# The opening stage of an attention and mixture-of-depths block: modulation in columns, first key and value pieces into four banks, loads and stack copies in another order

## The reference, cut to what matters

```python
x: (8, 1024, 512); c: (8, 512); wmod: (512, 6*512)
mod = (silu(c) @ wmod).reshape(8, 6, 1, -1)
sa, ca, ga, sb, cb, gb = mod[:, 0], ..., mod[:, 5]
ga = (2 * (ga >= 0) - 1) * maximum(abs(ga), 0.25)      # gb likewise
h = layernorm(x) * (1 + ca) + sa
x = x + ga * attention(h)        # 16 "heads": q, k, v = h @ W + b, reshaped to (b, 16, 32, 1024)
                                 # scores k^T v * temperature, softmax, then q times the probabilities
h = layernorm(x) * (1 + cb) + sb
x = x + gb * ffn(h)              # half of the tokens, chosen by a router score, go through W1, gelu, W2
```

## Time and profile before

| | us |
|---|---|
| median of 3 timed runs | 2418.35 (2418.11 to 2418.71) |
| the profiled execution's own time | 2416.8 |
| its span in the trace | 2415.1 |
| PE busy | 2273.9 (94% of the span) |
| DVE busy | 1911.6 (79%) |
| ACT busy | 1478.1 (61%) |
| POOL busy | 1371.5 (57%) |

### The profile page before, as it was taken

How to read it: one execution, slowest core, us unless ns; L and a number is a source line. 1 busy time by engine, 2 the same in 40 slices (tenths; PEclk the granted TensorE clock), 3 DMA queues, 4 the chain that set the end, 5 groups by cost and what they waited for, 6 DMA issues and landing times.

```text
span 2415.1 us, 41301 instructions
## 1 busy us (share of the span) xinstructions
PE 2273.9 (94%) x12772; PEld 887.0 (37%) x12772; DVE 1911.6 (79%) x2806; ACT 1478.1 (61%) x2616; POOL 1371.5 (57%) x1205
## 2 busy tenths in 40 slices
PE   6999999999999999999999999897989999999996
PEld 2333333333333333333333333231334444444442
DVE  5899899999999999999999999998744543554432
ACT  1788888888888888888888887777311111111110
POOL 4566676666756667666666666554344452543531
PEclk9999999999999999999999999999999999999998
DMA  6233333233333333323233333223612021111100
GB/s 214 68 92 77 79 82 88 72 91 72 76 87 77 84 73 90 82 70 96 67 80 97 72 79 75 67 61 97 157 44 66 22 59 52 32 57 44 57 23 18
DMA packets 123771, 180.83 MB, mean 75 GB/s; under 512 B 44112, under 2 KB 44112, under 8 KB 123480
## 3 DMA queue, kind: packets, MB, share of 16 engines
q1 hardware_dynamic: 113760, 152.30, 25.8%
q0 software_dynamic: 9728, 25.23, 3.4%
HBM read 67.17 MB, written 43.16 MB: 46 GB/s over the span
## 4 chain that ended last, share of the span: by engine, by line
PE 64%; DVE 17%; issue 8%; POOL 5%; ACT 3%; DMA 2%; SPq 1%; DVEq 0%; POOLq 0%; ACTq 0%
PE sc L558 13%; PE acc L605 13%; PE sc L747 12%; PE sc L734 12%; DVE nmax L981 10%; PE pj L568 7%; PE pj L580 5%; POOL x L1320 3%; DVE qn L1042 2%; ACT probs L810 2%; DVE stats L1024 1%; DMA room<-in_L_ffn_W 1%; PE sc L591 1%; POOL sel_rows L120 1%; DVE rinv L1037 1%
## 5 line engine op out<-in xcount | busy, mean ns | idle before, releaser
L810 ACT ACTIVATE probs<-sc,nmax 128x1024 f32<-128x1024 f32 x1024 | 1136.7, 1114 | 276.2 <-DVE nmax L981 254.8
L981 DVE TENSOR_REDUCE nmax<-sc 128x1 f32<-128x1024 f32 x1024 | 1212.6, 1215 | 61.1 <-PE sc L558 55.1
L605 PE MATMUL acc<-probs,qn 128*32 128x512 f32 x4136 | 556.7, 611 | 9.8 <-DVE x L1019 7.3
L883 ACT ACTIVATE probs<-sc,b_col 128x512 f32<-128x512 f32 x128 | 87.9, 687 | 561.6 <-PE sc L734 498.7
L568 PE MATMUL pj<-room 128*128 128x512 f16 x1536 | 395.6, 381 | 0.4 <-ACT qT L800 0.4
L747 PE MATMUL sc<-room,probs 128*128 128x512 f16 x1536 | 353.9, 380 | 8.0 <-DVE probs L1171 8.0
L558 PE MATMUL sc<-room 128*128 128x512 f16 x1024 | 310.3, 385 | 38.3 <-ACT probs L810 27.9
L558 PE MATMUL sc<-stacks 128*128 128x512 f16 x1024 | 309.5, 384 | 31.4 <-ACT probs L810 30.8
L1169 DVE CAST probs<-probs 128x512 f16<-128x512 f32 x128 | 64.6, 505 | 332.6 <-ACT probs L883 315.9
L747 PEld LDWEIGHTS sc<-room,probs 128*128 128x128 f16 x1536 | 150.0, 98 | 190.5 <-issue 7.4
L568 PEld LDWEIGHTS pj<-room 128*128 128x128 f16 x1536 | 150.2, 98 | 188.2 <-issue 9.1
(11 more groups left out here) (147 smaller groups left out, 2369.2 us busy)
## 6 DMA issues: line engine op xcount, KB each, us to landing
room<-room SPq DMA_DIRECT2D x512, 64.0 KB, 2.0
stacks<-room SPq DMA_DIRECT2D x512, 64.0 KB
h_rows<-hbuf SPq DMA_DIRECT2D x132, 128.0 KB, 2.3
out<-base SPq DMA_DIRECT2D x132, 128.0 KB, 2.5
room<-in_L_attn_x SPq DMA_DIRECT2D x96, 128.0 KB, 2.7
rows<-mod_rows SPq DMA_DIRECT2D x32, 256.0 KB, 4.1
room<-in_L_ffn_W SPq DMA_DIRECT2D x8, 1024.0 KB, 5.2
probs<-in_L_wmod SPq DMA_DIRECT2D x4, 1024.0 KB, 7.9
```

The lines of the kernel that those rows point to most:

```text
L605: mm = nc.tensor.matmul(acc[at:at + DH, :], qn[:, (p // 2) % 2, p % 2, h2, :], probs[:, (2 * p + h2) % PROBS, half * D:(half + 1) * D], st ...
L810: nc.scalar.activation(probs[:, u % PROBS, :], slot(g, ring_at(p, h2)), ACT.Exp, bias=nmax[:, u % PROBS:u % PROBS + 1], accum_out=rsum[:, ...
L883: nc.scalar.activation(g32[:, f % 2, :], ff[f % 2], ACT.Gelu_apprx_tanh, bias=b1_col[:, f:f + 1], scale=1.0 / WS).then_inc(gelu_done, 1)
L981: nc.vector.tensor_reduce(nmax[:, u % PROBS:u % PROBS + 1], slot(g, ring_at(p, h2)), AX.X, ALU.max, negate=True).then_inc(max_done, 1)
```

## The change

On the modulation: the weights of `modulate` become the blocks of the modulation matrix (128x128 each) and `cT` (128x8) streams past them, so that the result comes out in columns (128 partitions by 8 batches, `mod_cols` in bank 0 of `sc`) with no turn back. There are 16 matmuls for each `modulate` in place of 4. silu is made in columns after the transposes of c. DVE reads `mod_now` and `mod_table` straight from `mod_cols`. The four later vectors are gathered in `mod_c` (with the gates worked out in columns), turned to 32 rows by four transposes between the two query slices, and copied once to `mod_b`.

On keys, values and queries: the first four slices go to four banks and wait for no evacuation; modulate(2) stands between slices 1 and 2, modulate(3) to (5) behind the transposes of group 1; the two query slices go to two banks.

On the loads: bk and the temperatures (one DMA of 16 numbers to every partition, then four small DVE copies) come right after modulation matrix 1 and have a semaphore of their own; then Wk, group 1, matrix 2, Wv, bv, bq, Wq, group 2, matrices 3 to 5, and the router row last. b1 is loaded after the modulation rows are stored. The stack copies wait for `s_wsplit` 4 and go by halves: keys of heads 0, 1, values of heads 0, 1, keys of heads 2, 3, values of heads 2, 3. POOL no longer waits for `s_wsplit` 6, and waits for the last loads (`s_in` 3 x 16: bv, bq and the router row) before value slice kk = 2. DVE does the statistics of group 1 ahead of the splits of Wv and Wq.

```diff
+        mod_cols = sc[:, 0, 0:6 * CC * B].rearrange("p (j c b) -> p j c b", j=6, c=CC)
+        mod_rows_ps = sc[0:4 * B, 1, 0:D]
+        kv_first = [pj[:], sc[:, 1, 0:D], sc[:, 1, D:2 * D], acc[:]]
+        q_first = [pj[:], acc[:]]
@@ sync
             load_x(0, 0)
             stage_mod(0)
             stage_mod(1)
-            for k, w in enumerate((Wk, Wv)):
-                sp.dma_start(w_stage[k], ...).then_inc(s_w[k], 16)
-            sp.dma_start(bk_stage, bk.partition_broadcast(P)).then_inc(s_in, 16)
+            sp.dma_start(bk_stage, bk.partition_broadcast(P)).then_inc(s_bk, 16)
+            sp.dma_start(temp_all[:], temperature.rearrange("h a b -> (h a b)").partition_broadcast(P)).then_inc(s_bk, 16)
+            stage_w(0, Wk)
+            load_x(1, 1)
+            stage_mod(2)
+            stage_w(1, Wv)
             sp.dma_start(v_bias[:], bv.partition_broadcast(P)).then_inc(s_in, 16)
-            sp.dma_start(router_row[:], w_router.partition_broadcast(P)).then_inc(s_in, 16)
                 sp.dma_start(bq_col[:], bq.rearrange("(c p) -> p c", p=P)).then_inc(s_in, 16)
-                sp.dma_start(b1_col[:], b1.rearrange("(f p) -> p f", p=P)).then_inc(s_b, 16)
-                for hq in range(HG):
-                    sp.dma_start(temp_col[DH * hq:DH * (hq + 1), :], t_hq[hq].partition_broadcast(DH)).then_inc(s_in, 16)
-            stage_mod(2)
-            sp.dma_start(w_stage[2], Wq.rearrange("(c p) n -> p c n", p=P)).then_inc(s_w[2], 16)
-            load_x(1, 1)
+            stage_w(2, Wq)
+            load_x(2, 2)
             for j in range(3, 6):
                 stage_mod(j)
-            load_x(2, 2)
+            sp.dma_start(router_row[:], w_router.partition_broadcast(P)).then_inc(s_in, 16)
...
-            sp.wait_ge(s_wsplit, 6)
-            replicate(0, 0, 2)
-            replicate(0, 1, 4)
+            sp.wait_ge(s_wsplit, 4)
+            for heads in (range(0, HG // 2), range(HG // 2, HG)):
+                replicate(0, 0, 2, heads)
+                replicate(0, 1, 4, heads)
             sp.wait_ge(s_modv, 1)
             (store of the modulation rows), then
+                sp.dma_start(b1_col[:], b1.rearrange("(f p) -> p f", p=P)).then_inc(s_b, 16)
@@ tensor
             def modulate(j):
                 pe.wait_ge(s_wm[j], 16)
                 for cc in range(CC):
-                    mm = nc.tensor.matmul(mod_bank(j % 4), cT[:, cc, :], wm_stage[j][:, cc, :], start=(cc == 0), stop=(cc == CC - 1))
+                    for ci in range(CC):
+                        mm = nc.tensor.matmul(mod_cols[:, j, cc], wm_stage[j][:, ci, cc * P:(cc + 1) * P], cT[:, ci, :],
+                                              start=(ci == 0), stop=(ci == CC - 1))
                 mm.then_inc(s_mod, 1)
...
             modulate(0)
             modulate(1)
-            pe.wait_ge(s_mt, 1)
-            for k in range(2 * CC):
-                mm = nc.tensor.transpose(pj[:, k * B:(k + 1) * B], src, ident[0:B, 0:B])
             pe.wait_ge(s_xhat, 1)
             transposes(sc[:, 2, :])
+            pe.wait_ge(s_ht, 1)
+            keys_or_values(0)
+            keys_or_values(1)
+            pe.wait_ge(s_table, 1)
             modulate(2)
-            (four times: kv_slice(0, kk) behind kv_evac kk, then modulate(3 + kk))
+            keys_or_values(2)
+            pe.wait_ge(acc_free, 1)
+            keys_or_values(3)
             pe.wait_ge(t_evac, 1)
             pe.wait_ge(s_xhat, 2)
             transposes(sc[:, 2, :])
+            for j in range(3, 6):
+                modulate(j)
             pe.wait_ge(kv_evac, 4)
             pe.wait_ge(s_wsplit, 6)
-            whole(q_slice(0, 0))
-            pe.wait_ge(q_evac, 1)
-            whole(q_slice(0, 1))
+            whole(q_slice(0, 0, q_first[0]))
+            pe.wait_ge(s_v, 10)
+            for cc in range(CC):
+                mm = nc.tensor.transpose(mod_rows_ps[:, cc * P:(cc + 1) * P], mod_c[:, cc].rearrange("p b r -> p (b r)"), ident[:])
+            mm.then_inc(s_ct, 1)
+            whole(q_slice(0, 1, q_first[1]))
             pe.wait_ge(q_evac, 2)
             pe.wait_ge(t_evac, 2)
-            pe.wait_ge(s_modc, 1)
+            pe.wait_ge(s_modv, 1)
             pe.wait_ge(qn_done, 1)
             products(NQ)
@@ vector
+            dve.wait_ge(s_mod, 2), then mod_now and mod_table from mod_cols (6 small instructions)
+            split_w(0, wk16); dve.wait_ge(s_bk, 32); 4 copies to temp_col; tempw_col; k_bias (4)
+            statistics of group 1; split_w(1, wv16); split_w(2, wq16)
+            dve.wait_ge(s_mod, 6); 4 copies to mod_c; the two gates on [128, 4, 8] tiles
+            dve.wait_ge(s_ct, 2)
+            nc.vector.tensor_copy(mod_b, mod_rows_ps).then_inc(s_modv, 1)
@@ gpsimd
-            pool.wait_ge(s_wsplit, 6)
             normed_x(1, 2)
             pool.wait_ge(s_bias, 2)
             for kk in range(4):
+                if kk == 2:
+                    pool.wait_ge(s_in, 3 * 16)
                 split_kv(0, kk, kk + 1)
```

More of the change, by code:

```diff
@@ L414, in _ @@
+            sp.dma_start(temp_all[:], temperature.rearrange("h a b -> (h a b)").partition_broadcast(P)).then_inc(s_bk, 16)
[3 more added lines that the diff above has]
+            stage_w(1, Wv)
             sp.dma_start(v_bias[:], bv.partition_broadcast(P)).then_inc(s_in, 16)
-            sp.dma_start(router_row[:], w_router.partition_broadcast(P)).then_inc(s_in, 16)
-            with nc.allow_non_contiguous_dma(reason="512 biases and 16 temperatures, once"):
+            with nc.allow_non_contiguous_dma(reason="512 biases, once"):
@@ L424, in _, with replicate @@
-            load_x(1, 1)
+            stage_w(2, Wq)
+            load_x(2, 2)
             for j in range(3, 6):
                 stage_mod(j)
-            load_x(2, 2)
-            def replicate(m_par, k, split_count):
+            sp.dma_start(router_row[:], w_router.partition_broadcast(P)).then_inc(s_in, 16)
+            def replicate(m_par, k, split_count, heads=range(HG)):
                 src, parts = ((k16, (0, 0, 1, 1)), (v16, (0, 1, 0, 1)))[k]
                 sp.wait_ge(kv_split, split_count)
-                for hq in range(HG):
+                for hq in heads:
@@ L782, in evac_kv @@
                     act.wait_ge(kv_split, free)
[L783 removed]
+                nc.scalar.activation(kv32[kk % 2][:], src, ACT.Identity,
                                      scale=tempw_col[:, g:g + 1] if kk < 2 else 1.0 / WS).then_inc(kv_evac, 1)
@@ L793, in evac_t, with evac_q @@
                 return a
-            def evac_q(par, s, count):
+            def evac_q(par, s, count, src=pj[:]):
                 act.wait_ge(q_pe, count)
@@ L960, in _ @@
-            nc.vector.tensor_copy(mod_table[:, 0:B, :], tab).then_inc(s_table, 1)
-            for k, (w16, st) in enumerate(zip((wk16, wv16, wq16), w_stage)):
+            for j, add in ((0, 1.0), (1, 0.0)):
+                last = nc.vector.tensor_scalar(mod_now[:, j * CC:(j + 1) * CC], mod_cols[:, j, :, 0], add, None, ALU.add)
+            last.then_inc(s_now, 1)
+            for j, add in ((0, 1.0), (1, 0.0)):
+                part = slice(j * CC, (j + 1) * CC)
+                nc.vector.tensor_scalar(mod_table[:, B, part], mod_cols[:, j, :, B - 1], add, None, ALU.add)
+                last = nc.vector.tensor_scalar(mod_table[:, 0:B, part].rearrange("p b c -> p c b"), mod_cols[:, j], add, None, ALU.add)
@@ L967, in _ @@
                                                op0=ALU.mult, op1=ALU.subtract).then_inc(s_wsplit, 1)
-                if k == 0:
-                    dve.wait_ge(s_in, 8 * 16)
-                    nc.vector.tensor_scalar(tempw_col[:], temp_col[:], 1.0 / WS, None, ALU.mult).then_inc(s_bias, 1)
-                    for g in range(GB):
-                        last = nc.vector.tensor_scalar(k_bias[:, g, :], bk_stage, temp_col[:, g:g + 1], None, ALU.mult)
-                    last.then_inc(s_bias, 1)
+            split_w(0, wk16)
@@ new lines, in _ @@
+            dve.wait_ge(s_bk, 2 * 16)
+            for hq in range(HG):
+                part = slice(DH * hq, DH * (hq + 1))
+                last = nc.vector.tensor_copy(temp_col[part], temp_all[part].rearrange("p (g q) -> p q g", q=HG)[:, hq])
+            last.then_inc(s_temp, 1)
+            dve.wait_ge(s_temp, 1)
+            nc.vector.tensor_scalar(tempw_col[:], temp_col[:], 1.0 / WS, None, ALU.mult).then_inc(s_bias, 1)
+            for g in range(GB):
+                last = nc.vector.tensor_scalar(k_bias[:, g, :], bk_stage, temp_col[:, g:g + 1], None, ALU.mult)
@@ L977, in row_max @@
+            last.then_inc(s_bias, 1)
+            dve.wait_ge(s_xhat, 1)
+            for s in range(SUBS):
+                stats_of_x(1, s, 64)
+            aggregate(2)
+            split_w(1, wv16)
+            split_w(2, wq16)
             def row_max(b, g, p, h2):
```

122 lines of the change are left out of this document (52 added, 70 removed).

## The result

| | before | changed |
|---|---|---|
| median of 6 runs, us | 2417.75 (2412.75 to 2418.71) | 2425.67 (2424.21 to 2431.32) |
| span of the profiled execution | 2415.1 | 2424.6 |
| first score, in the trace | 66.83 | 75.58 |
| from there to the end of the span | 2348.3 | 2349.0 |

A forecast was written before the change was run, and what follows sets the result against it. PE, busy 94% of the span, bounds the kernel; only the first score's moment can move. 10.0 us from an earlier first score plus 1.5 from a warm PE make 11.5, so a median of 2407 us, range 2402 to 2416.

The forecast's parts named there:

- Start to the first modulation: Opening: silu is done well before matrix 0 lands at 8.4 us, so modulation begins at 8.5 us (8.87 before).
- The price of a pass: Each modulate: 32 f32 passes at 0.09 us, 2.9 us in all (3.60 before); 0.15 a pass at half clock.
- Modulations 0 and 1, the clock: First two modulations: 3.4 us at half clock, then full clock; they end at 15.6 us, tokens split at 22.7.
- over 4.8 was to prove me wrong: Sign against the forecast: modulations that took over 4.8 us each.
- PE from there: PE from the split tokens through slices, modulations 2 to 5 and query slices: first score at 56.8 us, against 66.83.
- What hides the rest: Transfers, POOL's new wait, SP's queue and DVE's work ahead of the first score: all covered by PE's 56.8 us.
- the cover of the router row: POOL's wait before value slice 2: last load in by 38 to 39.5 us, value stack at 51.6, five us of cover.
- First pair at full clock: After the first score: PE arrives warm, so a pair less its projection piece takes 1.97 us; 1.5 us gained.
- C: Rival, chance 0.17: the clock falls in modulations 3 to 5, half their passes at 0.15 us; 2409.5 to 2413 us.
- D: Rival, chance 0.10: weight load not hidden, a pass costs 0.12 to 0.16 us; 2416 us (2412 to 2421).
- E: Rival, chance 0.05: load and stream one behind the other, 0.20 us a pass, 6.4 us a modulate; 2428 us.
- Faster by the rest: Ahead of the first score: new order and banks, the 5.7 us of the 11.5 left beside the cheaper modulation.

The follow-up runs named there:

- e1: The changed kernel with the modulation in rows again, all else of the change kept; 2409.59 us, ratio 0.9972 to the kernel before.
- e6: The changed kernel with the thin passes of modulations 2 to 5 mixed among wide slice matmuls; 2413.31 us, ratio 0.9997 to the kernel before.
- e5: The changed kernel with blocks of extra matmuls, results unused, ahead of the first query slice to price single passes; 2493.27 us in all.

## Why the prediction was wrong

*Start to the first modulation*: right. silu was done at 4.3, the first thin pass came at 8.65 (8.5 forecast).

*The price of a pass*: mis-sized. I took 0.09 near L628's 0.074; it is 0.108 to 0.111. L628 loads 128 columns on 8 partitions in transposes; L591 loads 128 partitions and was the row to go by. I read 0.136 off it, with the tail of the last one in it, and kept it only as an upper bound; its second run, eight from 55.28 with the next instruction at 56.16, gives 0.110. At 0.108 alone the 192 passes would cost 3.5 us over my sum, and 2410.5 would have been the forecast.
The Trainium skill (TensorE: Matmul & The Clock Gate, LDWEIGHTS) has a formula that gives 107 ns for 128 columns; the runs agree, in f32 and at full clock, and where I had the row speak against it, I was wrong. The same page of the Trainium skill (The mechanism, in Part 3) lets a load overlap with running matmuls only on other rows of the array; the runs contradict that, as 8 and 128 streamed columns cost the same 0.111.

*Modulations 0 and 1, the clock*: this is the step that failed. "So 3.4 us at 0.15 (23 passes), 41 at 0.09" assumes that thin passes bring the clock up as wide ones do. They don't: all 64 ran at 0.216, and 15.6 became 22.5, 6.9 each where over 4.8 was to prove me wrong. The half-clock price was wrong as well, 0.15 by a ratio of 1.7 of short blocks, where it is twice 0.108. And the row that I took the 3.4 from was read roughly: 16 passes of L620 at full clock take 7.03 (as in e1 from 45.20), so 8.42 is some three passes at half speed over 2.7 us.

*PE from there*: the clock fell again under the thin passes, and the wide slices behind them paid too. The first slice ran at half clock for all of its 5.30 us, where I had it back after 3.6. Against my terms, from the split tokens on: first slice 5.30 (4.4), modulation 2 3.47 (2.9), slice 3 4.18 (2.7), modulations 3 to 5 17.13 (8.7), first query slice 4.29 (2.8). That is 12.9 us over; the tokens themselves were 7.1 late (29.77 for 22.7); the rest came in 1.2 under. 56.8 became 75.6. Of the 20 us over, the price of the 192 passes at full clock explains 3.5; the rest is the clock.

*What hides the rest*: the cover of the router row held (41.4, not 39.5, and needed at 48.9), at an estimate that left out that POOL and DVE hold each other up. *First pair at full clock*: right, 2.07 us from the first score to the first projection piece (77.65 in the chain; 1.97 forecast) and no half clock.

*The rivals*: C's mechanism came true, and with it a part of D: the load sets the price, but at 0.108, under D's 0.12 to 0.16, and the stream does hide beside it. I had each with the other at my own value, and C with half of the 96 passes slow and the opening spared. C's reason, "96 thin passes stream little", applied word for word to the 64 passes of the opening, and I didn't apply it there. With 0.108 for a pass, twice that at half clock, and C's clock in the opening and in the 96 passes, the sum comes out past the point at which the change loses. E's 2428 lies near the measured time, but by luck: it comes from load and stream one behind the other, 0.20 a pass at full clock, and that the prices exclude.

*Faster by the rest*: about right. With the modulation left in rows the order and banks gain 7 us net. In my 11.5 the cheaper modulation had some 6 (the tokens 3.0 earlier, and four modulations at 0.7 less), which leaves 5.7 for them.

## What to carry to other kernels

A small f32 product is not made cheap by giving it the wide side as weight: it pays for each 128x128 block as much as for 128 streamed columns, and a long run of such passes costs the clock, for itself and for what comes next. If it must be done so, put 512-wide matmuls between the passes (e6); f16 weights would be cheaper by the price of a pass, but no run here computes with them. When two rivals share a cause, price them together and in every stretch where the cause is present. And a wait that looks needless between VectorE and GpSimd may be what keeps the two apart, as that for `s_wsplit` 6 was.

## What the runs showed of the hardware that I had not expected

- TensorE's clock fell 3.1 us into a block of f32 passes with 8 streamed columns that kept PE and PEld busy without a gap; with one 512-column matmul to four such passes it stayed full for 11.5 us, with one of 256 columns it fell (e5, e6). Behind 32 passes that streamed 128 columns it stayed full, behind 32 that streamed 8 it fell (e5).
- The granted clock column can be wrong at the start of a trace, until the first change: 1.00 from 8 to 35 us in the changed kernel beside passes of 0.216 and wide matmuls of 0.44, twice their price.
- An f32 pass with a full weight costs 0.111 us with 8 or 128 columns streamed, the f16 one with 8 columns streamed 0.025 (e5).
- GpSimd took 3.34 us for two numbers per partition while VectorE split weights, and VectorE 2.01 us for one 32x4 copy (four took 3.32) while GpSimd split tokens (the changed kernel; e1 has the same 3.34).
